# Self-attention values on 64x32 tiles in float32, outputs of a tile copied at once

## The chip, the cores and the metric

One core of a Trainium2 chip. The metric is device time in microseconds (us) of one execution of the whole kernel. Engines: PE is TensorE (PEld its weight loads), DVE is VectorE, ACT is ScalarE, POOL is GpSimd, SP is SyncE.

## What is computed

A layer over x of 32 batches x 64 tokens x 512, with a context of 32 x 512 x 384: cross-attention, causal self-attention, then a feed-forward block on half of the tokens. The change is in the second line:

```python
x = x + xattn(layernorm(x), ctx, mask, Wq, Wk, Wv, Wo)      # 16 heads of 32
x = x + attn(layernorm(x), wq, wk, wv, wo)                  # below
x = x + ffn(layernorm(x), w_router, W1, b1, W2, b2)         # top half of the tokens

def attn(x, wq, wk, wv, wo):          # 16 heads of 32, 64 queries, 64 keys
    q, k, v = heads(x @ wq), heads(x @ wk), heads(x @ wv)
    q, k = rope(q), rope(k)
    s = where(causal, q @ k.T / sqrt(32), -inf)
    return merge(softmax(s) @ v) @ wo
```

## The kernel before

Every engine has its own instruction stream, written out by hand, and they meet in semaphores. The order of the work is the order in these streams. The three blocks follow each other; their edges overlap. The self-attention works on 16 tiles of 128 tokens, two batches each. PSUM, where TensorE writes, has 8 banks (`bank[0]` to `bank[7]`).

Precision: a projection is made of three float32r products, high x high, high x low and low x high (`project`, line 955). The high part is a copy rounded to float32r (ScalarE), the low part is what is left (VectorE). The scores (`scores`, line 977) are one product in plain float32; TensorE records each such matmul twice. The values before (`values`, line 995) are float32r again: for each pair of 128-column blocks, each batch and each of the three products, the 64 rows of a batch hold 128 columns of v as the stationary operand and the probabilities of 4 heads (256 columns) move. Of the result only the part that belongs to the head is used. It lies in banks 4 to 7, where the scores are too. For this the probabilities, transposed into banks 0 and 1, are copied to `pb_h` by ScalarE and corrected to `pb_l` by VectorE (line 1225), two halves a tile; v is copied to `v_h` and corrected to `v_l` (line 1194); and the outputs are picked out head row by head row: four copies to `o_h` (32 partitions each, `outputs`, line 1083) and four corrections to `o_l` (line 1190) a tile, which the output projection (line 969) takes.

A step t of `pe3` (line 1007) holds, in this order: query projection of tile t+1 (bank 2); transposes of the rotated queries and keys of tile t (lines 1017 and 1022, banks 0 and 1); key projection of t+1 (bank 3); scores of t (banks 4 to 7); probability transposes of t-1 (line 991, banks 0 and 1); output projection of t-2 (bank 2); token transposes of t+2 (line 966, bank 3); values of t-1 (banks 4 to 7); value projection of t+1 (bank 1). In a step VectorE (`dve3`) has: value correction, two output corrections of t-2, rotation of the queries (lines 1141, 1149), rotation of the keys, mask (line 1216), two probability corrections, maximum (line 1229), residual add and statistics of t-2, token correction (line 1180), two output corrections of t-1, sum (line 1242) and reciprocal (line 1246). ScalarE (`act3`) has the copies that go with these, the layer norm (line 410) and the exponential (line 1133). GpSimd (`pool3`) has the sums of the rotation (lines 1253, 1257), subtracts the maximum (line 1262) and multiplies by the reciprocal (line 1266), which makes the probabilities.

`steps` (line 1269) runs t = 0 and 1 written out, then a hardware loop that runs a body of six steps twice, then t = 14 written out (for GpSimd also 15). In step 14 ScalarE also makes the deviations of 12 tiles (two table loads) and normalizes four tiles for the next block (`act_normalize`, line 1440). The last tile is in `pe_end`, `act_end` and `dve_end` (from line 1493): there the self-attention's last products are mixed with the beginning of the next block, which is the router's dot products (`dve_dot`), their spread over a batch (`pe_spread`, line 1459), comparison and one-hot (`dve_compare`, `dve_one_hot`), gathers of the chosen tokens (`pe_gather`, line 1468) and splits of the first feed-forward weights (`act_split`). `settle` (line 58) is an increment of a semaphore that nobody waits for, put after a wait.

## Time and profile before

| | |
|---|---|
| median of 3 runs | 1393.96 us (1391.40 to 1397.39) |
| the profiled execution | 1394.26 us |
| its span | 1392.5 us |
| busy in the span: TensorE, VectorE, ScalarE, GpSimd | 97%, 52%, 54%, 39% |
| granted TensorE clock, mean | 0.994 of full speed |
| stages in the trace (us from the span's start) | cross-attention to about 896, self-attention 896 to 1177, feed-forward from 1185 |

The profile is of one execution; its rows give busy times and, for each wait, who ended it. In the timeline a row may join several instructions; its second number then runs from the first one's start to the last one's end. TensorE's instructions overlap, so the distance between two starts is what an instruction costs, and its recorded duration is longer. In the chain of waits, pieces follow each other end to end.

### The profile page before, as it was taken

How to read it: one execution, taken by the hardware profiler on the slowest of the kernel's cores; microseconds unless marked ns; L12 is line 12 of the kernel's file. 1: busy time of each engine (PE TensorE's matmuls, PEld its weight loads, DVE VectorE, ACT ScalarE, POOL GpSimd, SP SyncE). 2: the span in 40 equal slices, each digit the busy share in tenths (PEclk: the TensorE clock that was granted, in tenths of full speed). 3: DMA queues.
4: the chain of work that ended last, by engine and by line, in shares of the span. 5: the costliest groups of instructions: out<-in, count | busy, mean ns of one | idle time of the engine just before them, and what ended most of it. 6: DMA issues, size and time to landing. Idle time of an engine off the chain costs nothing.

```text
span 1392.5 us, 32047 instructions
## 1 busy us (share of the span) xinstructions
PE 1356.0 (97%) x12344; PEld 1071.5 (77%) x12344; DVE 729.7 (52%) x1784; ACT 758.7 (54%) x1458; POOL 543.7 (39%) x284
## 2 busy tenths in 40 slices
PE   7999999999999999999999999989999997999998
PEld 5777777777777777777777777778888886878686
DVE  4244454454454444444444444468878889732323
ACT  5455665665665665665665666644444466442231
POOL 6543423323323323323324325634344334375342
PEclk9999999999999999999999999999999999999999
DMA  7011111111111111111111130100000002233131
GB/s 251 25 58 34 50 32 32 49 32 32 49 32 32 49 32 32 49 32 32 49 32 32 49 122 13 55 1 2 2 3 1 1 1 92 61 91 98 68 136 61
DMA packets 39340, 66.31 MB, mean 48 GB/s; under 512 B 4208, under 2 KB 8560, under 8 KB 39280
## 3 DMA queue, kind: packets, MB, share of 16 engines
q1 hardware_dynamic: 38848, 64.67, 14.4%
q8 instruction: 44, 0.72, 0.2%
q10 hardware_dynamic: 432, 0.79, 0.2%
q14 instruction: 16, 0.13, 0.0%
HBM read 61.25 MB, written 4.19 MB: 47 GB/s over the span
## 4 chain that ended last, share of the span: by engine, by line
PE 89%; DVE 2%; ACT 1%; issue 1%; POOL 1%; POOLq 0%; DVEq 0%; ACTq 0%
PE psum L204 38%; PE psum L958 9%; PE psum L252 8%; PE psum L1849 6%; PE psum L1820 6%; PE psum L222 5%; PE psum L240 5%; PE psum L973 3%; PE psum L261 3%; PE psum L1002 2%; PE psum L991 1%; PE psum L983 1%; PE psum L1831 1%; PE psum L1476 1%; PE psum L1022 0%
## 5 line engine op out<-in xcount | busy, mean ns | idle before, releaser
L300 ACT ACTIVATE PT<-psum 128x512 f32<-128x512 f32 x256 | 153.2, 598 | 230.0 <-PE psum L252 230.0
L287 ACT ACTIVATE prob<-prob,nmx 128x512 f32<-128x512 f32 x256 | 182.6, 714 | 94.4 <-DVE nmx L342 94.4
L356 DVE COPY V<-psum 128x512 f32<-128x512 f32 x128 | 88.6, 692 | 230.2 <-PE psum L204 230.2
L342 DVE CUSTOM_DVE_ANT_0 prob<-psum,mbias 128x512 f32<-128x512 f32 x256 | 165.5, 684 | 67.0 <-PE psum L222 67.0
L293 ACT ACTIVATE prob<-prob,rinv 128x512 f32<-128x512 f32 x256 | 182.7, 714 | 0.0
L489 POOL TENSOR_SCALAR ctx_a<-ctx_r 128x1536 fp32r<-128x1536 f32 x16 | 65.4, 4090 | 265.2 <-PE psum L204 265.0
L489 POOL TENSOR_SCALAR ctx_b<-ctx_r 128x1536 fp32r<-128x1536 f32 x16 | 65.5, 4091 | 251.6 <-PE psum L204 235.4
L252 PEld LDWEIGHTS psum<-ident,prob 128*128 128x128 f32 x1024 | 127.9, 141 | 34.6 <-issue 1.5
L252 PE MATMUL psum<-ident,prob 128*128 128x128 f32 x1024 | 153.7, 272 | 0.5 <-ACT PT L300 0.4
L204 PE MATMUL psum<-wv_h,ctx_b 128*128 128x512 f32 x384 | 144.7, 418 | 0.0
L204 PE MATMUL psum<-wv_h,ctx_a 128*128 128x512 f32 x384 | 142.2, 412 | 1.2 <-DVE K L356 1.2
L356 DVE COPY K<-psum 128x512 f32<-128x512 f32 x128 | 88.4, 691 | 96.1 <-PE psum L204 78.9
L204 PE MATMUL psum<-ctx_b,wk_h 128*128 128x512 f32 x384 | 128.3, 401 | 2.2 <-DVE x_l L1180 2.2
L204 PE MATMUL psum<-ctx_a,wk_h 128*128 128x512 f32 x384 | 127.2, 399 | 0.0
L1363 POOL TENSOR_TENSOR w_l<-w_r,w_h 128x1024 fp32r<-128x1024 f32 x32 | 77.2, 2412 | 74.0 <-ACT w_h L1358 64.7
L240 PEld LDWEIGHTS psum<-PT,V 128*32 128x32 f32 x4096 | 60.1, 110 | 51.3 <-DVE V L356 22.7
L204 PEld LDWEIGHTS psum<-ctx_b,wk_h 128*128 128x128 f32 x384 | 72.3, 188 | 19.9 <-DVE x_l L1180 2.4
L204 PEld LDWEIGHTS psum<-ctx_a,wk_h 128*128 128x128 f32 x384 | 72.0, 188 | 18.1 <-DVE V L356 0.8
L204 PEld LDWEIGHTS psum<-wv_h,ctx_a 128*128 128x128 f32 x384 | 72.2, 188 | 14.8 <-DVE K L356 1.6
L204 PEld LDWEIGHTS psum<-wv_h,ctx_b 128*128 128x128 f32 x384 | 72.5, 189 | 13.1
L204 PE MATMUL psum<-wv_l,ctx_b 128*128 128x512 f32 x192 | 75.4, 393 | 0.0
L204 PE MATMUL psum<-ctx_b,wk_l 128*128 128x512 f32 x192 | 75.4, 393 | 0.0
(225 smaller groups left out, 2968.8 us busy)
## 6 DMA issues: line engine op xcount, KB each, us to landing
ctx_r<-in_ctx SPq DMA_DIRECT2D x32, 768.0 KB, 4.6
w_r<-in_L_ffn_W SPq DMA_DIRECT2D x64, 256.0 KB, 2.8
xres<-in_x SPq DMA_DIRECT2D x16, 256.0 KB, 2.7
out<-tok SPq DMA_DIRECT2D x13, 256.0 KB, 3.7
tok<-in_x SPq DMA_DIRECT2D x3, 1024.0 KB, 12.0
...
```

Of the source, the lines that this page charges most:

```text
L204: ins = pe.matmul(KV_bank[m % 2], stat, mov, start=(c == 0 and n == 0), stop=(c == CT - 1 and n == PRODUCTS - 1))
L240: ins = pe.matmul(place[r * HD:(r + 1) * HD, c * SQ:(c + 1) * SQ], V_sb[:, b, kt, h:h + HD], PT[:, r, kt, c * SQ:(c + 1) * SQ], start=(kt ...
L252: ins = pe.transpose(T_bank[:, kt * P:(kt + 1) * P], prob[:, r, kt * P:(kt + 1) * P], ident[:])
L287: act.activation(prob[:, r, :], prob[:, r, :], ACT.Exp, bias=nmx[:, r:r + 1], scale=-1.0, accum_out=rsum[:, r:r + 1]).then_inc(s_ex, 1)
L293: act.activation(prob[:, r, :], prob[:, r, :], ACT.Copy, scale=rinv[:, r:r + 1]).then_inc(s_pn, 1)
L300: act.activation(PT[:, r, :, :].rearrange("p k n -> p (k n)"), T_bank, ACT.Copy).then_inc(s_Pt, 1)
L342: dve.tensor_tensor_reduce(prob[:, r, :], S_bank[r], mbias[:, b, :], 1.0, 3.0e38, ALU.add, ALU.min, nmx[:, r:r + 1]).then_inc(s_mx, 1)
L356: dve.tensor_copy(item_place(q, m), KV_bank[m % 2]).then_inc(s_KVe, 1)
L489: pool.tensor_scalar(y[:, 0], ctx_r[:], 1.0, None, ALU.mult).then_inc(s_cx, 1)
L958: ins = pe.matmul(b, y[:, k, :], w[:, k, :], start=(k == 0 and i == 0), stop=(k == DT - 1 and i == PRODUCTS - 1))
L1820: ins = pe.matmul(h_bank[e % 2], w[:, e, 0, k * P:(k + 1) * P], y[:, k, cols], start=(k == 0 and i == 0), stop=(k == DT - 1 and i == PRODU ...
L1849: ins = pe.matmul(y_bank[t], h[:, e % 2, t * P:(t + 1) * P], w[:, e, 1, :], start=(isinstance(f, int) and f == 0 and i == 0), stop=(isinst ...
```

## The change

The transposed probabilities and v are kept as plain float32 (`pT`, `v_s`), with one ScalarE copy each and no correction. The values of a tile become 32 float32 matmuls, one for each head and batch: the batch's 64 rows x the head's 32 columns of v are stationary, the head's 64 probability columns move, at tile position (64 b, 32 r). Consecutive matmuls alternate between the two row halves; the halves write banks 0 and 1. All four head rows of the output then hold only what is used, so one ScalarE copy and one VectorE correction of 128 partitions take the whole tile; `o_h` and `o_l` get two buffers. On TensorE the values of t-1 move from after the token transposes to right behind the scores of t, the probability transposes of t-1 move into the middle of the key projection, and the value projection into bank 1 now waits for the output correction of t-1. ScalarE copies the output before the token copy; VectorE corrects it after the maximum, and the statistics of t-2 move behind the token correction. The loop runs a body of two steps six times. In the last tile the probability transposes of tile 14 move ahead of the scores, both waiting output projections and the first spread move ahead of tile 15's probabilities, and `act_normalize(act, 1)` moves behind the exponential; the last outputs go to banks 4 and 5.

```diff
--- before.py
+++ after.py
@@ -918,31 +918,30 @@
...
-        pb_h = m("pb_h", [P, 2, 2, 4, SQ], F32R)
+        pT = m("pT", [P, 2, 4, 2, SQ], F32)
...
+        v_s = Map(nc, PT_end - 8 * 1024)("v", [P, 2, D], F32)
...
-        v_h = m("v_h", [P, 3, D], F32R)
...
-        o_h, o_l = m("o_h", [P, DT, BPG, SQ], F32R), m("o_l", [P, DT, BPG, SQ], F32R)
+        o_h, o_l = m("o_h", [P, 2, DT, BPG, SQ], F32R), m("o_l", [P, 2, DT, BPG, SQ], F32R)
...
-        pb_l, v_l = m("pb_l", [P, 2, 2, 4, SQ], F32R), m("v_l", [P, 3, D], F32R)
@@ -992,27 +991,25 @@
...
-        def values(pe, buf, h):
-
-            for n in (2 * h, 2 * h + 1):
-                cols = slice(n % 2 * 4 * SQ, (n % 2 + 1) * 4 * SQ)
-                for i, (v, p) in enumerate(((v_h, pb_h), (v_l, pb_h), (v_h, pb_l))):
+        def values(pe, buf, first_bank=0):
+
+            for n in range(DT):
+                for r in range(4):
                     for b in range(BPG):
-                        rows = slice(b * SQ, (b + 1) * SQ)
-                        ins = pe.matmul(bank[4 + 2 * b + h][:, cols], v[rows, buf, n * P:(n + 1) * P],
-                                        p[rows, h, n % 2, :, :].rearrange("p a c -> p (a c)"),
-                                        start=(i == 0), stop=(i == PRODUCTS - 1), tile_position=(b * SQ, 0))
+                        rows, h = slice(b * SQ, (b + 1) * SQ), n * P + r * HD
+                        ins = pe.matmul(bank[first_bank + b][head_rows(r), n * SQ:(n + 1) * SQ], v_s[rows, buf, h:h + HD],
+                                        pT[rows, n // 2, r, n % 2, :], start=True, stop=True,
+                                        tile_position=(b * SQ, r * HD))
             return ins
...
                 pe.wait_ge(s3_aq, t + 1)
-                if has(t - 2):
-                    pe.wait_ge(s3_pd, 2 * t - 2)
...
@@ -1022,54 +1019,50 @@
...
             if has(t + 1):
-                project(pe, bank[3], x3_h[:, nxt, :, :], x3_l[:, nxt, :, :], kw_h, kw_l).then_inc(s3_K, 1)
+                project(pe, bank[3], x3_h[:, nxt, :, :], x3_l[:, nxt, :, :], kw_h, kw_l, (0, 1))
+            if has(t - 1):
+                pe.wait_ge(s3_pn, t)
+                pe.wait_ge(s3_qa, t + 1)
+                pe.wait_ge(s3_kT, t + 1)
+                for h in range(2):
+                    probabilities(pe, nxt, h).then_inc(s3_PT, 1)
+            if has(t + 1):
+                project(pe, bank[3], x3_h[:, nxt, :, :], x3_l[:, nxt, :, :], kw_h, kw_l, (2, 3)).then_inc(s3_K, 1)
             if has(t):
                 pe.wait_ge(s3_kT, t + 1)
                 pe.wait_ge(s3_qa, t + 1)
-                at_least(pe, s3_od, 4 * t - 4)
+                at_least(pe, s3_ms, t)
                 if isinstance(t, int) and t == 0:
                     pe.wait_ge(s_x1, G + 1)
                 scores(pe).then_inc(s3_S, 1)
             if has(t - 1):
-                pe.wait_ge(s3_pn, t)
-                if has(t):
-                    pe.wait_ge(s3_qa, t + 1)
-                    pe.wait_ge(s3_kT, t + 1)
-                for h in range(2):
-                    probabilities(pe, nxt, h).then_inc(s3_PT, 1)
+                pe.wait_ge(s3_pa, 2 * t)
+                settle(pe)
+                values(pe, nxt).then_inc(s3_PV, 1)
             if has(t - 2):
                 pe.wait_ge(s3_rq, 2 * t + 4)
                 if isinstance(t, int) and t == 2:
                     pe.wait_ge(s3_wd, 1)
-                pe.wait_ge(s3_od, 4 * t - 4)
-                output_projection(pe).then_inc(s3_Wo, 1)
+                pe.wait_ge(s3_od, t - 1)
+                output_projection(pe, par).then_inc(s3_Wo, 1)
             if has(t + 2):
                 pe.wait_ge(s3_rk, 2 * t + 4)
                 pe_x(pe, t + 2, bank[3])
-            if has(t - 1):
-                pe.wait_ge(s3_v, t)
-                if has(t):
-                    pe.wait_ge(s3_ms, t + 1)
-                for h in range(2):
-                    pe.wait_ge(s3_pd, 2 * t - 1 + h)
-                    ins = values(pe, (tri - 1) % 3, h)
-                ins.then_inc(s3_PV, 1)
             if has(t + 1):
+                at_least(pe, s3_od, t)
                 project(pe, bank[1], x3_h[:, nxt, :, :], x3_l[:, nxt, :, :], vw_h, vw_l).then_inc(s3_V, 1)
...
-        def o_block(r):
-
-            src = psum[head_rows(r), 4:8, :].rearrange("p g c -> p (g c)")
-            src = src.rearrange("p (b n h q) -> p n b h q", b=BPG, n=DT, h=4)[:, :, :, r, :]
...
+        def o_block(buf, first_bank=0):
+
+            src = psum[:, first_bank:first_bank + BPG, 0:DT * SQ].rearrange("p b (n q) -> p b n q", n=DT)
+            return src, o_h[:, buf].rearrange("p n b q -> p b n q"), o_l[:, buf].rearrange("p n b q -> p b n q")
+
+        def p_place(h):
+
+            return pT[:, h].rearrange("p r c q -> p (r c q)")
@@ -1077,21 +1070,12 @@
...
             if has(t):
                 act.wait_ge(s3_V, t + 1)
-                if isinstance(t, int):
-                    at_least(act, s3_PV, t - 2)
-                else:
-                    act.wait_ge(s3_PT, 2 * t - 2)
-                copy(v_h[:, tri, :], bank[1]).then_inc(s3_vh, 1)
@@ -1108,31 +1092,28 @@
...
-            if isinstance(t, int) and t == G - 2:
-                act_deviations(act, MOST)
-                act.activation(warm[:], epsb[:], ACT.Exp)
             if has(t - 1):
                 at_least(act, s3_PV, t - 1)
                 for h in range(2):
                     act.wait_ge(s3_PT, 2 * t - 1 + h)
-                    src, high, _ = p_block(h)
-                    copy(high, src).then_inc(s3_pa, 1)
+                    copy(p_place(h), bank[h]).then_inc(s3_pa, 1)
             if isinstance(t, int) and t == G - 2:
+                act_deviations(act, MOST)
+                act.activation(warm[:], epsb[:], ACT.Exp)
                 act.wait_ge(s3_K, G)
                 act.wait_ge(s4_nm, 1)
                 act_normalize(act, 0)
+            if has(t - 1):
+                at_least(act, s3_Wo, t - 2)
+                act.wait_ge(s3_PV, t)
+                src, high, _ = o_block(1 - par)
+                copy(high, src).then_inc(s3_oa, 1)
             if has(t + 2):
                 act_x(act, t + 2, par, bank[3])
-            if has(t - 1):
-                at_least(act, s3_Wo, t - 1)
-                act.wait_ge(s3_PV, t)
-                outputs((0, 1))
             if has(t):
                 act.wait_ge(s3_su, t + 1)
                 s_ = sm[:, par].rearrange("p a b c d -> p (a b c d)")
                 act.activation(s_, s_, ACT.Exp).then_inc(s3_ex, 1)
-            if has(t - 1):
-                outputs((2, 3))
 
@@ -1181,19 +1162,20 @@
...
-            if has(t):
-                dve.wait_ge(s3_vh, t + 1)
-                dve.tensor_tensor(v_l[:, tri, :], bank[1], v_h[:, tri, :].bitcast(F32), ALU.subtract).then_inc(s3_v, 1)
-            if has(t - 2):
-                outputs(t - 2, (2, 3))
...
+        def dve_o(dve, tile, buf, first_bank=0):
+
+            src, high, low = o_block(buf, first_bank)
+            dve.wait_ge(s3_oa, tile + 1)
+            dve.tensor_tensor(low, src, high.bitcast(F32), ALU.subtract).then_inc(s3_od, 1)
@@ -1213,30 +1195,20 @@
...
-                                         .broadcast_to([P, 4, 4 * SQ]), op0=ALU.mult, op1=ALU.add).then_inc(s3_ms, 1)
-            if has(t - 1):
-                at_least(dve, s3_PV, t - 1)
-                for h in range(2):
-                    src, high, low = p_block(h)
-                    dve.wait_ge(s3_pa, 2 * (t - 1) + h + 1)
-                    dve.tensor_tensor(low, src, high.bitcast(F32), ALU.subtract).then_inc(s3_pd, 1)
-            if has(t):
...
+            if has(t - 1):
+                dve_o(dve, t - 1, 1 - par)
             if has(t - 2):
                 dve.wait_ge(s3_Wo, t - 1)
                 dve.tensor_tensor(one_tile(t - 2), bank[2], one_tile(t - 2), ALU.add).then_inc(s3_x, 1)
-                next_stats(dve, t - 2)
             if has(t + 2):
                 dve_x(dve, t + 2, par, bank[3])
-            if has(t - 1):
-                at_least(dve, s3_Wo, t - 1)
-                outputs(t - 1, (0, 1))
+            if has(t - 2):
+                next_stats(dve, t - 2)
             if has(t):
                 dve.wait_ge(s3_ex, t + 1)
@@ -1269,12 +1241,12 @@
...
-                step(eng, t, t % 2, t % 3)
-            with eng.Fori(0, (G - 4) // 6) as h:
-                for i in range(6):
-                    step(eng, 6 * h + 2 + i, i % 2, (2 + i) % 3)
+                step(eng, t, t % 2)
+            with eng.Fori(1, G // 2 - 1) as h:
+                for i in range(2):
+                    step(eng, 2 * h + i, i)
             for t in range(G - 2, end):
-                step(eng, t, t % 2, t % 3)
@@ -1501,39 +1474,35 @@
...
-            pe.wait_ge(s3_kT, G)
+            pe.wait_ge(s3_pn, LAST)
             pe.wait_ge(s3_qa, G)
-            pe.wait_ge(s3_od, 4 * (LAST - 1))
-            scores(pe).then_inc(s3_S, 1)
-            pe.wait_ge(s3_pn, LAST)
             pe.wait_ge(s3_v, G)
             for h in range(2):
                 probabilities(pe, 1 - PAR, h).then_inc(s3_PT, 1)
+            pe.wait_ge(s3_kT, G)
+            pe.wait_ge(s3_ms, LAST)
+            scores(pe).then_inc(s3_S, 1)
+            pe.wait_ge(s3_pa, 2 * LAST)
+            values(pe, 1 - PAR).then_inc(s3_PV, 1)
             pe.wait_ge(s3_x, LAST - 2)
-            output_projection(pe).then_inc(s3_Wo, 1)
-            pe.wait_ge(s3_ms, G)
-            for h in range(2):
-                pe.wait_ge(s3_pd, 2 * LAST - 1 + h)
-                ins = values(pe, (TRI - 1) % 3, h)
-            ins.then_inc(s3_PV, 1)
+            output_projection(pe, PAR).then_inc(s3_Wo, 1)
+            pe.wait_ge(s3_x, LAST - 1)
+            pe.wait_ge(s3_od, LAST)
+            output_projection(pe, 1 - PAR).then_inc(s3_Wo, 1)
+            pe_spread(pe, 0)
 
             pe.wait_ge(s3_pn, G)
             for h in range(2):
                 probabilities(pe, PAR, h).then_inc(s3_PT, 1)
-            pe.wait_ge(s3_x, LAST - 1)
-            pe.wait_ge(s3_od, 4 * LAST)
-            output_projection(pe).then_inc(s3_Wo, 1)
-            pe_spread(pe, 0)
-            for h in range(2):
-                pe.wait_ge(s3_pd, 2 * G - 1 + h)
-                ins = values(pe, TRI, h)
-            ins.then_inc(s3_PV, 1)
+            pe.wait_ge(s3_ms, G)
+            pe.wait_ge(s3_pa, 2 * G)
+            values(pe, PAR, LAST_BANK).then_inc(s3_PV, 1)
             pe_gather(pe, 0, 0)
             pe_gather(pe, 0, 1)
             pe_spread(pe, 1)
             pe.wait_ge(s3_x, LAST)
@@ -1542,40 +1511,36 @@
...
-            act_normalize(act, 1)
...
+            src, high, _ = o_block(1 - PAR)
+            copy(high, src).then_inc(s3_oa, 1)
             act.wait_ge(s3_su, G)
             last = sm[:, PAR].rearrange("p a b c d -> p (a b c d)")
             act.activation(last, last, ACT.Exp).then_inc(s3_ex, 1)
-            act.wait_ge(s3_Wo, LAST - 1)
-            act.wait_ge(s3_PV, LAST)
-            for r in range(4):
-                src, high, _ = o_block(r)
-                copy(high, src).then_inc(s3_oa, 1)
+            act_normalize(act, 1)
 
             for f in range(3):
                 act_split(act, f)
...
+                copy(p_place(h), bank[h]).then_inc(s3_pa, 1)
+            act.wait_ge(s3_Wo, LAST - 1)
+            act.wait_ge(s3_PV, G)
+            src, high, _ = o_block(PAR, LAST_BANK)
+            copy(high, src).then_inc(s3_oa, 1)
             act_normalize(act, 2)
-            act.wait_ge(s3_Wo, LAST)
-            act.wait_ge(s3_PV, G)
-            for r in range(4):
-                src, high, _ = o_block(r)
-                copy(high, src).then_inc(s3_oa, 1)
@@ -1588,40 +1553,21 @@
...
-            outputs(LAST - 2, (2, 3))
-            dve.wait_ge(s3_vh, G)
-            dve.tensor_tensor(v_l[:, TRI, :], bank[1], v_h[:, TRI, :].bitcast(F32), ALU.subtract).then_inc(s3_v, 1)
...
-            dve.wait_ge(s3_PV, LAST - 1)
-            low_probabilities(LAST - 1)
+            dve_o(dve, LAST - 1, 1 - PAR)
             add(LAST - 2)
@@ -1630,20 +1576,16 @@
...
-            dve.wait_ge(s3_Wo, LAST - 1)
-            outputs(LAST - 1, range(4))
...
             dve_diagonal(dve, 0)
-            dve.wait_ge(s3_PV, LAST)
-            low_probabilities(LAST)
...
             dve_diagonal(dve, 1)
-            outputs(LAST, range(4))
+            dve_o(dve, LAST, PAR, LAST_BANK)
...
```

## Rows read from the trace of the kernel before

**Rows 1.** The page's first part: busy time, share of the span, instructions.
```profile
PE 1356.0 (97%) x12344; PEld 1071.5 (77%) x12344; DVE 729.7 (52%) x1784; ACT 758.7 (54%) x1458; POOL 543.7 (39%) x284
```

**Rows 2.** Chain of waits, steady loop: start us, us, engine, written tile, line, count.
```profile
1033.73 5.91 PE psum L958 x24
...
1098.57 5.71 PE psum L958 x24
...
1112.67 0.44 PE psum L966 x4
...
1113.10 1.63 PE psum L1002 x24
```

**Rows 3.** Timeline, TensorE, one step: start us, us from first start to last end.
```profile
1039.91 0.60 PE L1022 MATMUL psum<-ident,k_r 128*128 128x128 f32 x4
...
1040.58 0.39 PE L958 MATMUL psum<-ak_l,x_h 128*128 128x512 f32 x1
...
1043.22 1.01 PE L983 MATMUL psum<-k_T,q_T 32*64 32x64 f32 x64
...
1044.16 1.09 PE L991 MATMUL psum<-ident,sm 128*128 128x128 f32 x8
...
1045.33 0.40 PE L973 MATMUL psum<-ao_l,o_h 128*128 128x512 f32 x1
...
1047.86 0.60 PE L966 MATMUL psum<-ident,xn 128*128 128x128 f32 x4
...
1050.36 0.39 PE L958 MATMUL psum<-av_l,x_h 128*128 128x512 f32 x1
```

**Rows 4.** Timeline, TensorE, cross-attention.
```profile
501.44 1.10 PE L240 MATMUL psum<-PT,V 128*32 128x64 f32 x64
...
502.81 0.40 PE L204 MATMUL psum<-ctx_b,wk_l 128*128 128x512 f32 x1
```

**Rows 5.** Timeline, VectorE, tiles 0 and 1.
```profile
917.85 0.69 DVE L1141 TENSOR_TENSOR r_cos<-psum,rope 128x512 f32<-128x512 f32 x1 [2.30 <-PE psum L958]
...
919.12 1.22 DVE L1216 SCALAR_TENSOR_TENSOR sm<-psum,cmask 128x1024 f32<-128x1024 f32 x1
...
920.37 1.22 DVE L1229 TENSOR_REDUCE mx<-sm 128x16 f32<-128x1024 f32 x1
...
921.50 0.68 DVE L1180 TENSOR_TENSOR x_l<-psum,x_h 128x512 fp32r<-128x512 f32 x1
...
931.84 0.69 DVE L1141 TENSOR_TENSOR r_cos<-psum,rope 128x512 f32<-128x512 f32 x1 [1.23 <-POOL q_r L1253]
```

**Rows 6.** Timeline, TensorE, start of the self-attention.
```profile
927.00 0.63 PE L1022 MATMUL psum<-ident,k_r 128*128 128x128 f32 x4 [1.14 <-DVE v_l L1194]
...
936.70 0.50 PE L958 MATMUL psum<-av_h,x_h 128*128 128x512 f32 x1
```

**Rows 7.** Timeline, ScalarE, end of the self-attention.
```profile
1142.85 2.93 ACT L1443 ACTIVATE xn<-tok,nmr,rs 128x512 f32<-128x512 f32 x4
...
1157.83 1.06 ACT L1560 ACTIVATE sm<-sm 128x1024 f32<-128x1024 f32 x1
...
1161.23 2.95 ACT L1358 ACTIVATE w_h<-w_r 128x1024 fp32r<-128x1024 f32 x3
```

**Rows 8.** Timeline, GpSimd, end of the self-attention.
```profile
1150.73 1.91 POOL L1266 TENSOR_TENSOR sm<-sm,rc 128x1024 f32<-128x1024 f32 x1 [3.20 <-DVE rc L1246]
...
1160.61 1.90 POOL L1266 TENSOR_TENSOR sm<-sm,rc 128x1024 f32<-128x1024 f32 x1 [2.81 <-DVE rc L1632]
```

**Rows 9.** Timeline, TensorE, end of the self-attention.
```profile
1152.14 1.00 PE L983 MATMUL psum<-k_T,q_T 32*64 32x64 f32 x64 [1.69 <-DVE o_l L1595]
...
1171.39 3.84 PE L1476 MATMUL psum<-oh,xn 128*128 128x128 f32 x32 [1.51 <-DVE oh L1430]
...
1177.14 0.47 PE L973 MATMUL psum<-ao_h,o_h 128*128 128x512 f32 x1 [1.48 <-DVE o_l L1595]
...
1179.98 2.25 PE L1476 MATMUL psum<-oh,xn 128*128 128x128 f32 x18
```

81 lines of the change are left out of this document (31 added, 50 removed).

## The prediction

> **What bounds the kernel now.** I read the page's first part, then the chain of waits from 890 to 1215 us (self-attention and its two seams), then each engine's timeline there. TensorE is busy for 97% of the span [rows 1]. In the chain, one tile of the steady loop is TensorE alone: 16.16 us from one value projection to the next (1098.57 to 1113.10 + 1.63), of which the values product, line 1002, holds 1.63 [rows 2]. No other engine stands in the chain from 936 to 1146 us. So in the loop only what shortens TensorE's own sequence counts. VectorE and ScalarE time that comes free is worth nothing there; it is worth something at the seams, where TensorE waits for them.
>
> **The values product.** Before: 24 matmuls of 256 columns in float32r. After: 32 matmuls of 64 columns in float32 on 64x32 tiles. A float32 matmul is recorded twice, as the scores are (64 records for 32 matmuls). Recorded durations overlap, so I work with distances from start to start.
> - Taken out: from the first token transpose (1047.86) to the second matmul of the value projection (1050.36) it is 2.50 us, with the values between [rows 3]. Straight from four transposes to a projection it is 1039.91 to 1040.58, or 0.67 [rows 3]. So 1.83 leave.
> - Put in: today it is 0.94 from the scores to the probability transposes (1043.22 to 1044.16), and 1.17 from there to the output projection's second matmul (1045.33), 2.11 in all [rows 3]. New: the eight transposes stand inside the key projection and add 0.88 (four take 0.44 in the chain [rows 2]); the split itself costs nothing more, as a projection follows transposes without a gap already. Scores to values 0.94, as to the transposes now. Values to output projection: the trace has no 64x32 tile with 64 columns. The nearest row is the cross-attention's product on 128x32 tiles, also 64 records of 64 columns: from its first to the second matmul behind it 501.44 to 502.81, or 1.37 [rows 4]. Sum 3.19, or 1.08 more.
> - Net: -0.75 us for each tile. The cheap bound is the pace of the scores, 64 columns on 32x64 tiles (0.94 to what follows and 0.32 to its second matmul: 1.26), net -0.86. The dear bound: if the two row halves didn't overlap, the 64 records, 0.88 us at the cross-attention's pace, take twice that, net +0.13. The scores alternate their row groups matmul by matmul as the new product alternates its halves, and they overlap; so I take 1.37.
> - The no-op that line 61 adds on TensorE's queue ahead of the values: at nothing, since the queue runs ahead of the array; bound 0 to +0.15 a tile.
>
> **Are the new waits covered?** Take S, the first start of the scores. VectorE has the key rotation at S+0.11, the mask at +1.38, the maximum at +2.63 and whatever follows at +3.76: so it was for tile 0, which has no probability correction between (917.85, 919.12, 920.37, 921.50 [rows 5]; its scores began at 917.74). What follows is now the one output correction, 0.69 long, which TensorE sees at about S+4.6. The value projection, which now waits for it since the outputs sit in banks 0 and 1, would start at 0.94 + 1.37 + 2.53 (1045.33 to 1047.86) + 0.35 = S+5.2. Margin 0.6 us. The probability transposes wait for ScalarE's key copy, which I put half a microsecond ahead of them. Then what goes from the other engines (two probability, one value and three output corrections on VectorE, three copies on ScalarE, per tile) is worth nothing in the loop: TensorE covered it. If that cover went, the next in line would be this same output correction.
>
> **Loop turns.** The loop of six steps jumps back once, and there the chain shows 5.91 where it has 5.71 elsewhere [rows 2]. A loop of two steps jumps back five times: 4 x 0.2 = +0.8.
>
> **Start.** TensorE waited 1.14 us for the value correction at 927.00 [rows 6]. That goes, but tile 0's probabilities are now wanted 3 us sooner than GpSimd has them, which gives about 0.95 back. What decides is the value projection of tile 2, at 936.70 [rows 6]. It now waits for mask, maximum and output correction behind a key rotation that GpSimd held until 931.84 [rows 5], or until 931.25 with VectorE free 0.6 sooner: 3.65 + 0.69 + 0.13 later is 935.7 to 936.3. I take -0.7, bound 0 to -1.0.
>
> **Steady part.** Values of tiles 1 to 12: 12 x -0.75 = -9.0.
>
> **End.** In the last loop-like step ScalarE normalizes four tiles, 2.93 us from 1142.85 [rows 7], ahead of the output copy, as before. The last value projection now waits for the correction behind that copy: about +2.0 on TensorE. It delays nothing, since GpSimd has tile 14's probabilities only at 1150.73 + 1.91 = 1152.6 [rows 8], as before. On the old clock, from there:
> - The transposes of tile 14 go first, so the last scores start at 1153.6 for 1152.14 [rows 9]. From the scores to the end of GpSimd's last multiply it was 1162.51 - 1152.14 = 10.4 [rows 8, 9]; tile 15's probabilities come at 1164.0, a loss of 1.5.
> - In exchange both output projections that stood behind them, and the first spread, are done by then. The last exponential ended at 1158.9 [rows 7]; 1.5 later comes 1160.4. Behind it ScalarE has one normalization (2.93), the weight splits (2.95 [rows 7]) and two copies (1.09), no longer four output copies: last values at 1167.5, first gather at 1168.5 for 1171.39 [rows 9].
> - Gather and spread take 4.3; comparison and one-hot, 2.8 on VectorE, then start at once, where they stood behind four output corrections for which TensorE, too, waited 1.48 at 1177.14 [rows 9]. Second gather at about 1175.8 for 1179.98 [rows 9].
> - So -4.1, bound 0 to -6, as several chains meet here. Behind it the order is unchanged.
>
> **Sum.** -0.7 - 9.0 + 0.8 - 4.1 = -13.0 us. The profiled execution took 1394.26 (span 1392.5), 0.3 above the median of 1393.96; from the median, 1381.
>
> **A rule against it.** The scores' 64 records start 12.5 ns apart, (1.01 - 0.22)/63 [rows 3]. The Trainium skill (TensorEngine Tiling (Array Packing), Performance Considerations) says that a matmul costs about 60 cycles on top however few columns it has, and advises against tiling what is small already. By an estimate from that page, 64 records take 1.6 us at 2.4 GHz, as much as the old product; the trace agrees with it only if a float32 matmul counts once.
>
> **Rivals.**
> - A floor of some 26 ns for each record: 64 x 26 = 1.66 us for 0.88. The loop then gains nothing: -0.7 + 0.4 + 0.8 - 2.5 = -2.0, 1392. Both tiled products in the trace run at half that. (The page's rule, counted per record, is this case.) Chance 0.06.
> - Partly given back: the no-op and its wait drain TensorE between scores and values (12 x 0.15 = 1.8), the start gives nothing and the end 0 to -2, since ScalarE's long normalizations stand before what TensorE needs: -9.0 + 0.8 + 1.8 and 0 to -2 are -6.4 to -8.4, 1386 to 1388. For it: that seam is decided by waits less than 1 us apart. Chance 0.24.
> - Slower: row halves that alternate don't run side by side on 64-row tiles, each record takes 55 ns and the product 3.5 us. With a product of P us the sum is 12 (P - 1.63) + 2 (P - 0.88) - 0.7 + 0.8 - 4.1 = 14 P - 25.3 (two of the products lie on the end's path): +24, 1418. It passes zero at 28 ns a record and +7 us at 36. The scores' alternation speaks against it. Chance 0.05.
>
> **How the numbers follow.** The forecast keeps 0.65. A measurement of this kernel tells about 0.5%, 7 us, from no change; the forecast and most of the partial case lie below 1387: faster 0.81. The rest of it and the floor: same 0.14. Slower 0.05. The low end takes the cheap bound (12 x 0.11) and an end of -6, 1378, with 3 us for covers I did not see; the high end is the partial case's, with 1 us for the median's own place: 1375 to 1389.
>
> **What would show it.** In the chain a period of 15.4 us with values of 0.85 to 1.05 and no VectorE line; 2 us of waiting at the last value projection; the second gather 13 us sooner. A period over 15.8, or a value projection that waits for the output correction in each tile, would make it wrong.

## The result, and the profile after

The kernel after the change takes 1378.60 us (median of 4 executions, 1377.36 to 1379.07), beside 1393.03 us of the kernel before on the same chip (1391.40 to 1397.39): a ratio of 0.989 [0.9866, 0.9914], or 14.4 us less. The forecast was 1381 in a range of 1375 to 1389. The profiled execution took 1377.36 us, its span is 1374.9, its mean granted clock 0.995.

The page's first part, kernel after (compare [rows 1]):

```profile
PE 1341.6 (98%) x12984; PEld 1059.8 (77%) x12984; DVE 666.7 (48%) x1688; ACT 730.2 (53%) x1410; POOL 544.3 (40%) x284
```

VectorE lost 63.0 us of work (729.7 to 666.7) and ScalarE 28.5, about four times and twice what the kernel won, and TensorE is as full as it was. The time was won where TensorE's own sequence became shorter. The chain of waits in the steady loop of the kernel after (start us, us, engine, written tile, line, count; compare [rows 2]):

```profile
1043.08 5.54 PE psum L957 x24
...
1049.49 1.38 PE psum L957 x6
1050.88 0.87 PE psum L990 x8
1051.75 1.40 PE psum L957 x6
1053.14 0.94 PE psum L982 x56
1054.09 0.79 PE psum L1000 x53
1054.88 2.96 PE psum L972 x12
...
1058.28 1.85 PE psum L957 x8
```

The period, from one value projection's start to the next (1043.08 to 1058.28), is 15.20 us here and 15.19 over eleven steps, for 16.16. (The view ends inside the last row's piece; whole, it is 5.54, as at 1043.08.) The chain holds TensorE alone. The values (line 1000) hold 0.79 us for 1.63. The same step in TensorE's timeline (compare [rows 3]):

```profile
1053.08 1.01 PE L982 MATMUL psum<-k_T,q_T 32*64 32x64 f32 x64
1054.02 0.86 PE L1000 MATMUL psum<-pT,v 64*32 64x64 f32 x64
1054.81 0.50 PE L972 MATMUL psum<-ao_h,o_h 128*128 128x512 f32 x1
1055.14 0.40 PE L972 MATMUL psum<-ao_l,o_h 128*128 128x512 f32 x1
...
1057.68 0.60 PE L965 MATMUL psum<-ident,xn 128*128 128x128 f32 x4
1058.03 0.48 PE L957 MATMUL psum<-av_h,x_h 128*128 128x512 f32 x1
```

Scores to values is 0.94, as predicted, so the no-op ahead of the values costs nothing. From the first value matmul to the second matmul of the output projection it is 1.12 (1054.02 to 1055.14), where the prediction took 1.37. The records start (0.86 - 0.22)/63 = 10.2 ns apart. VectorE in that step, kernel after:

```profile
1054.45 1.22 DVE L1167 SCALAR_TENSOR_TENSOR sm<-psum,cmask 128x1024 f32<-128x1024 f32 x1
1055.70 1.22 DVE L1201 TENSOR_REDUCE mx<-sm 128x16 f32<-128x1024 f32 x1
1056.84 0.68 DVE L1176 TENSOR_TENSOR o_l<-psum,o_h 128x512 fp32r<-128x512 f32 x1
```

The output correction ends at 1057.5 and the value projection, which waits for it, starts at 1058.03: the margin is about half a microsecond.

At the start of the self-attention the value projection of tile 2 waits 2.32 us for the output correction, `o_l`. VectorE's key rotation, which stands with mask and maximum ahead of that correction, waits in turn for a GpSimd sum, `q_r`, that takes 3.39 us beside VectorE's `ao_l`, where it takes 1.27 elsewhere. This slow sum is not new: in the kernel before it takes 3.39 us at the same place (the last row below). Timelines of TensorE, GpSimd and VectorE, kernel after, then GpSimd, kernel before:

```profile
934.88 0.72 PE L957 MATMUL psum<-av_h,x_h 128*128 128x512 f32 x1 [2.32 <-DVE o_l L1176]
935.40 0.63 PE L957 MATMUL psum<-av_l,x_h 128*128 128x512 f32 x1
935.83 0.63 PE L957 MATMUL psum<-av_h,x_l 128*128 128x512 f32 x1
...
927.00 3.39 POOL L1225 TENSOR_TENSOR q_r<-r_cos,r_sin 128x512 f32<-128x512 f32 x1
...
926.98 2.28 DVE L1187 TENSOR_TENSOR ao_l<-ao_r,ao_h 128x2048 fp32r<-128x2048 f32 x1
...
928.35 3.39 POOL L1253 TENSOR_TENSOR q_r<-r_cos,r_sin 128x512 f32<-128x512 f32 x1
```

The matmuls behind the wait start 0.43 us apart instead of 0.23, for eight of them: TensorE is at half clock, 1.2 GHz (the granted clock from 936 to 938 us is 0.50). TensorE's timeline at the end of the self-attention (compare [rows 9]), with one VectorE row last; the row ahead of them all is the last key projection's last matmul in the kernel before, from which the end is measured further on:

```profile
1139.85 0.40 PE L958 MATMUL psum<-ak_h,x_l 128*128 128x512 f32 x1
...
1128.66 0.40 PE L957 MATMUL psum<-ak_h,x_l 128*128 128x512 f32 x1
...
1135.62 0.50 PE L957 MATMUL psum<-av_h,x_h 128*128 128x512 f32 x1 [1.87 <-DVE o_l L1176]
...
1141.45 1.06 PE L990 MATMUL psum<-ident,sm 128*128 128x128 f32 x8 [0.35 <-ACT q_T L1512]
1142.44 1.01 PE L982 MATMUL psum<-k_T,q_T 32*64 32x64 f32 x64
...
1153.57 1.22 PE L1437 MATMUL psum<-dg,same 128*128 128x256 f32 x2 [2.20 <-DVE dg L1375]
1154.58 1.91 PE L990 MATMUL psum<-ident,sm 128*128 128x128 f32 x8
1157.28 0.85 PE L1000 MATMUL psum<-pT,v 64*32 64x64 f32 x64 [0.78 <-ACT pT L1512]
1158.05 3.84 PE L1448 MATMUL psum<-oh,xn 128*128 128x128 f32 x32
...
1165.30 3.84 PE L1448 MATMUL psum<-oh,xn 128*128 128x128 f32 x32 [0.21 <-DVE oh L1402]
...
1151.52 2.00 DVE L1375 TENSOR_TENSOR dg<-fold,s_all 128x256 f32<-128x256 f32 x1
```

**Four stretches.** For every trace I took five starts of TensorE: the query projection of tile 1 (Q1), the value projections of tiles 2, 3 and 14 (V2, V3, V14), and the first matmul of the feed-forward's second weights (FF). V3 to V14 is eleven steady steps. All later readings go by this table (us; medians of all executions in the last column, each beside a kernel before of 1392.5 to 1394.2).

| kernel | Q1-V2 | V2-V3 | V3-V14 | V14-FF | Q1-FF | median |
|---|---|---|---|---|---|---|
| before | 25.44 | 16.16 | 177.96 | 61.85 | 281.41 | 1393.03 |
| before, second trace | 25.92 | 17.19 | 177.94 | 62.04 | 283.09 | 1393.73 |
| after | 24.97 | 16.80 | 167.07 | 59.48 | 268.32 | 1378.60 |
| product alone | 23.95 | 16.93 | 169.30 | 60.15 | 270.33 | 1378.87 |
| VectorE's work back | 26.03 | 17.82 | 167.08 | 60.21 | 271.14 | 1381.12 |
| row halves in turn | 24.97 | 16.88 | 168.67 | 61.17 | 271.69 | 1382.14 |
| six-step body | 24.98 | 16.79 | 167.85 | 59.06 | 268.68 | 1378.21 |
| weights' correction later | 24.09 | 16.79 | 167.09 | 60.75 | 268.72 | 1378.36 |
| output copy ahead, step 14 | 24.98 | 17.94 | 167.05 | 61.22 | 271.19 | 1378.46 |
| both | 24.10 | 16.80 | 167.05 | 59.97 | 267.92 | 1377.56 |
| output correction later | 26.18 | 18.57 | 175.25 | 61.84 | 281.84 | 1390.18 |
| start: output ahead | 22.83 | 16.22 | 167.07 | 59.37 | 265.49 | 1376.19 |
| start: weights in step 0 | 23.76 | 15.28 | 166.65 | 59.54 | 265.23 | 1375.71 |
| values twice | 24.99 | 17.39 | 173.89 | 63.31 | 279.58 | 1387.00 |

So of the 13.1 us between the first two profiled self-attentions, 10.9 lie in the eleven steady steps, 2.4 at the end, 0.5 at the start, and 0.6 are given back from V2 to V3. The spans differ by 17.6 us; the rest lies outside the self-attention and is taken up with the last experiment.

The last stretch is the least certain one. Five kernels with the same code behind V14 (after, six-step body, weights' correction later, and the two last placings at the start) have 59.06 to 60.75 us there. Two things differ from trace to trace: how long TensorE is at half clock, and an idle time in one of the last output projections (the profile calls it "issue": no engine is named), which is 0.16 us in the kernel after, 1.48 with VectorE's work back, 1.74 with the row halves in turn and 1.56 with the output correction later. Why it differs was not tried.

### The profile page after: what moved, and what is told of

Its sections match the earlier page's. It is cut to its first block, busy times and chain, and to the rows that moved or that the text cites. A ratio compares the mean times of both kernels' runs of the same rounds, so it can differ in the third digit from the quotient of the medians.

```text
span 1374.9 us, 33152 instructions
## 1 busy us (share of the span) xinstructions
PE 1341.6 (98%) x12984; PEld 1059.8 (77%) x12984; DVE 666.7 (48%) x1688; ACT 730.2 (53%) x1410; POOL 544.3 (40%) x284
## 4 chain that ended last, share of the span: by engine, by line
PE 89%; DVE 2%; ACT 2%; issue 1%; POOL 1%; POOLq 0%; DVEq 0%; ACTq 0%
PE psum L204 39%; PE psum L957 9%; PE psum L252 8%; PE psum L1791 6%; PE psum L1762 6%; PE psum L222 5%; PE psum L240 5%; PE psum L261 3%; PE psum L972 3%; PE psum L990 1%; PE psum L1448 1%; PE psum L982 1%; PE psum L1000 1%; PE psum L1773 1%; PE psum L1019 0%
```

## Experiments

### The product alone

The kernel before with the new product and what it needs (float32 `pT` and `v_s`, one output copy and correction), in the old order: values behind the token transposes, banks 4 and 5, body of six steps.

```diff
-                for h in range(2):
-                    pe.wait_ge(s3_pd, 2 * t - 1 + h)
-                    ins = values(pe, (tri - 1) % 3, h)
-                ins.then_inc(s3_PV, 1)
+                pe.wait_ge(s3_pa, 2 * t)
+                settle(pe)
+                values(pe, nxt).then_inc(s3_PV, 1)
```

> The kernel before with the new product alone: values in float32 on 64x32 tiles, still after the token transposes (banks 4 and 5), no corrections of probabilities and v, one copy and one correction of the output; TensorE's order, the loop of six steps and the order of the last tile stay. Theory (the product's own time pays, the moves only make room for it): from the rows of the changed kernel (0.20 to the first of its 64 records, 0.79 to what follows, 0.33 to the second matmul, for 2.50 with the old product) the period is 16.16 - 0.85 = 15.3 us, and the total 9 to 13 us below the kernel before. Rival (the new order and the two-buffer outputs carry the gain, since they take waits off the loop): the period stays above 15.9 and the total gains less than 4 us.

Measured: 1378.87 us (1378.40 to 1380.84), ratio 0.9899 [0.9883, 0.9916]. Chain of waits, product alone:

```profile
1030.21 0.60 issue
...
1042.63 0.79 PE psum L1002 x53
1043.42 5.70 PE psum L959 x24
...
1053.71 1.02 PE psum L992 x8
1054.74 2.77 PE psum L974 x12
...
1058.73 3.42 PE psum L959 x14
```

The period is 15.31 (1043.42 to 1058.73; the view ends inside the last piece), so the product brings 0.85 us a tile and the new order another 0.12. The 0.60 of "issue" at 1030.21 is the jump of the six-step body; that one step is 16.17. Moving the transposes and the values trades pieces almost evenly: transposes 1.02 to 0.87 and value and query projection 5.70 to 5.54, against 2.77 to 2.96 for the output projection. By the medians the product alone is the whole gain, within what can be told; between the two profiled self-attentions (270.33 and 268.32) the other changes bring 2.0 us. The end takes 60.15 here with the old order of the last tile, for 61.85 before and 59.48 after. That lies within what kernels with the new order vary by, so no run shows that the new order of the last tile gained anything.

### VectorE's work back in

The kernel after, with two extra rotations, one token correction and three statistics a step, into spare tiles: 3.8 us more of VectorE per step, in about the places of what was removed, but nothing more ahead of the output correction than the two rotations in the query part.

```diff
+                for i in range(2):
+                    dve.tensor_tensor(spare[i][:].rearrange("p (h i) -> p h i", h=HEADS), bank[2].rearrange("p (h i) -> p h i", h=HEADS),
+                                      rope[:, 0:1, :].broadcast_to([P, HEADS, HD]), ALU.mult)
...
+                dve.wait_ge(s3_xh, t + 3)
+                dve.tensor_tensor(spare[2][:], bank[3], x3_h[:, par].rearrange("p n c -> p (n c)").bitcast(F32), ALU.subtract)
...
+            if has(t - 2):
+                for i in range(3):
+                    dve.bn_stats(spare[3 + i][:, 0:6], one_tile(t - 2))
```

> The changed kernel with as much VectorE work as the change took out of a step: six operations of 0.6 to 0.7 us on spare tiles, put where the trace shows VectorE idle (two beside the query rotation, one beside the token correction, three behind the reciprocal). Theory (VectorE's freed time is worth nothing in the loop): period 15.19 us as in the changed kernel, total within 3 us of it. Rival (the freed time is what pays): the period goes back towards 16.16, total up by up to 12 us.

Measured: 1381.12 us (1378.79 to 1381.73), ratio 0.9906 [0.9889, 0.9924]. V3 to V14 is 167.08, the same as without: in the loop this time of VectorE's is worth nothing. The 2.8 us between the traces lie at the seams: 1.1 up to V2, where TensorE waits for VectorE's rotations (1.00 and 1.16 us for 0.50 and 0.61), 1.0 to V3 (a longer stretch at half clock), and 0.7 at the end, which isn't more than that stretch varies by.

### Row halves in turn

```diff
-            for n in range(DT):
-                for r in range(4):
-                    for b in range(BPG):
+            for b in range(BPG):
+                for n in range(DT):
+                    for r in range(4):
```

> The changed kernel with the two row halves of the values one after the other (batch loop outermost), so that consecutive matmuls no longer alternate between row halves. Theory 1 (the alternation keeps 8 tiles at work; 4 tiles alone run at the cross-attention's pace): the 64 records take 0.88 us for 0.64 (13.9 ns each for 10.2), +0.25 a tile, +3 to 4 us in all. Theory 2 (a fixed cost of each matmul sets the pace, not the tiles): 0.64 as before, no change.

Measured: 1382.14 us (1381.45 to 1383.03), ratio 0.992 [0.9904, 0.9937]. Timeline of TensorE, halves in turn:

```profile
1055.51 0.99 PE L1000 MATMUL psum<-pT,v 64*32 64x64 f32 x64
1056.43 0.51 PE L972 MATMUL psum<-ao_h,o_h 128*128 128x512 f32 x1
```

The product takes 0.92 from start to start for 0.79, and a steady step 0.145 us more (168.67 - 167.07, over eleven). The records start 12.3 ns apart ((0.99 - 0.22)/63 is 12.2; over all 16 tiles the trace has 12.3) for 10.2. So neither theory holds: alternating the halves is worth half of what the first one said, and no row shows which tiles run side by side. That the total is 3.5 us up, as the first theory had it, is luck: 1.6 lie in the eleven steps, and 1.7 at the end, where TensorE has the idle 1.74 us for which no engine is named. The 55 ns a record of the third rival are far off in either order.

### The body of the loop

```diff
-            with eng.Fori(1, G // 2 - 1) as h:
-                for i in range(2):
-                    step(eng, 2 * h + i, i)
+            with eng.Fori(0, (G - 4) // 6) as h:
+                for i in range(6):
+                    step(eng, 6 * h + 2 + i, i % 2)
```

> The changed kernel with the old loop, a body of six steps run twice. As predicted (each jump back costs 0.2 us): -0.8 us, with one step of 15.4 in the trace. Rival (a jump back of the two-step body costs nothing, as the even period of 15.19 in the trace of the changed kernel says; only the long body's jump costs): +0.2, one step of 15.4, total the same.

Measured: 1378.21 us (1377.15 to 1378.91), ratio 0.9888 [0.9871, 0.9904]. Chain of waits, six-step body:

```profile
1029.58 2.77 PE psum L957 x12
1032.35 0.48 issue
1032.83 3.00 PE psum L957 x12
...
1045.48 5.54 PE psum L957 x24
```

The long body's one jump costs 0.7 us (this step is 15.90, V3 to V14 is 0.78 more); the five jumps of the short body cost nothing that shows: its steps with and without a jump all take 15.15 to 15.20, and the long body's steps without one 15.19 to 15.22. The term of +0.8 has the wrong sign. At the level of the whole kernel the two can't be told apart.

### The output correction later

VectorE makes two more such corrections (of 0.6 us each, into spare tiles) ahead of the real one.

```diff
+            for i in range(2):
+                dve.tensor_tensor(spare[i][:].rearrange("p (n b q) -> p b n q", n=DT, b=BPG), src, high.bitcast(F32), ALU.subtract)
             dve.tensor_tensor(low, src, high.bitcast(F32), ALU.subtract).then_inc(s3_od, 1)
```

> The kernel after the change, with VectorE's o_l late by two more such subtractions (into spare tiles, about 0.6 us each, 1.2 us together) ahead of the real one, in every tile. It tests the prediction's margin: it put the new wait of the value projection for o_l 0.6 us clear of being felt (the trace of the changed kernel says 0.5). If so, the value projection starts 1.2 - 0.5 = about 0.7 us late in each step: period 15.9 instead of 15.19, time +8 to +10 us, 1387 to 1389, and the chain of waits now names VectorE's o_l in the loop. If the half clock follows such waits as at the start, more: up to +20. Rival (the wait is hidden by more than I say, because the projection is not what bounds): no change. Rival (any VectorE time counts): 1.2 x 14 = +17.

Measured: 1390.18 us (1388.15 to 1394.10), ratio 0.9984 [0.9972, 0.9996]. Chain of waits, correction later:

```profile
1048.61 1.12 DVE spare L1178 x2
...
1049.84 0.65 DVE o_l L1179
...
1050.54 5.77 PE psum L958 x24
```

VectorE now stands in the loop's chain, and the period is 15.93 (175.25 / 11), 0.74 more for 1.2 us of delay: the margin was 0.46, by a test that doesn't rest on reading when a semaphore is seen. It is the nearest limit in the loop. The median lies 1 to 3 us above what I expected. In the trace 5.3 us lie outside the eleven steps: 1.2 up to V2, 1.8 to V3 (the wait there is 3.52 us, and the stretch at half clock is longer) and 2.4 at the end, part of which is the idle time with no engine named. Two instructions, 1.2 us together, in the wrong place give back 11.6 of the 14.4 us.

### Values twice

```diff
-            for n in range(DT):
+            for n, c in [(n, DT + n) for n in range(DT)] + [(n, n) for n in range(DT)]:
...
-                        ins = pe.matmul(bank[first_bank + b][head_rows(r), n * SQ:(n + 1) * SQ], v_s[rows, buf, h:h + HD],
+                        ins = pe.matmul(bank[first_bank + b][head_rows(r), c * SQ:(c + 1) * SQ], v_s[rows, buf, h:h + HD],
```

> The kernel after the change, with the 64 value matmuls of each tile made twice, the first set into PSUM columns that nobody reads. It measures the disputed term, the price of 64 more such matmuls on tiles of 64 rows by 32 columns. The prediction took 1.37 us from the first of them to the next step's second matmul, and bounds of 26 to 55 ns a matmul record; the changed kernel's trace says 0.79 from the first value matmul to the first projection matmul, 10.2 ns each by the group's own length. If the pace is what counts: +0.65 to +0.79 a tile, period 15.84 to 15.98, and 16 x 0.65 to 0.79 = +10.4 to +12.6 us, 1389 to 1391.5. Rival (the pace of 12.5 ns that the scores have): +0.8, period 15.99. Rival (an entry cost of about 0.2 us is hidden in the first set only, so that a second costs more than its length): over +0.85.

Measured: 1387.00 us (1385.90 to 1391.64), ratio 0.9957 [0.9943, 0.9971]. Chain of waits, values twice:

```profile
1044.62 1.41 PE psum L1000 x91
...
1049.43 5.54 PE psum L957 x24
...
1065.25 5.54 PE psum L957 x24
```

64 further records cost 0.62 us a step (15.81 for 15.19; 6.82 over eleven steps): 9.7 ns each, just under the low end of what I expected, and the rest of the 0.79, 0.17 us, is paid once for the group. So the disputed term is 0.62 + 0.17, not the 0.88 and more that the cross-attention's rows suggested. The median rises by 8.4 us, less than the 10.4 to 12.6 I expected, while the profiled self-attention is 11.3 longer. The profiled execution, at 1390.14, is slower than the median and has a mean granted clock of 0.995 where the median one has 0.998, so the step is read from the trace and not from the median.

### The start: three placings

First the weights' correction (`ao_l`, 2.28 us) moves in step 1 from ahead of the key rotation to behind the token correction.

```diff
             if isinstance(t, int) and t == 1:
                 shifts(dve, slice(G - 2, G), 2)
-                dve.wait_ge(s3_wa, 1)
-                dve.tensor_tensor(ow_l[:], ow_r[:], ow_h[:].bitcast(F32), ALU.subtract).then_inc(s3_wd, 1)
...
                 dve_x(dve, t + 2, par, bank[3])
+            if isinstance(t, int) and t == 1:
+                dve.wait_ge(s3_wa, 1)
+                dve.tensor_tensor(ow_l[:], ow_r[:], ow_h[:].bitcast(F32), ALU.subtract).then_inc(s3_wd, 1)
```

> The kernel after the change, with one thing moved: in step 1 VectorE subtracts the high part of the self-attention output weights (128x2048, 2.28 us) after x_l of tile 3 instead of ahead of the rotation of K. In the changed kernel that subtraction ran beside GpSimd's q_r (3.39 us), which held back r_cos, the mask, o_l and with o_l the value projection of tile 2 (a 2.32 us wait), and TensorE's next matmuls were at half clock (12 of them in 7.39 us with Q's, 5.54 in a steady step). Theory (the start gave back what the change took in the steps): the wait falls under 0.5 us, the half clock goes with it, and the time falls by 2.3 + 1.85 = about 4 us, at least 2.5: 1374.5 to 1376 where the changed kernel gives 1378.6. Rival (something else ends there next: x_l of tile 3, or the subtraction now holds back the row sum and the next step's rotation): the value projection starts sooner, but the next query projection waits instead; gain 0 to 1.5 us. Second rival: the half clock is not caused by the wait, since it stays where the wait is gone; gain about 2.3.

Measured: 1378.36 us (1375.44 to 1379.52), ratio 0.9891 [0.9874, 0.9907]. The theory missed, and neither rival had the cause. GpSimd's sum is back at 1.27 us, but the wait only fell from 2.32 to 2.11, and the half clock stayed. Timelines of VectorE and TensorE, correction later:

```profile
932.53 1.22 DVE L1167 SCALAR_TENSOR_TENSOR sm<-psum,cmask 128x1024 f32<-128x1024 f32 x1
933.78 1.22 DVE L1199 TENSOR_REDUCE mx<-sm 128x16 f32<-128x1024 f32 x1
934.91 0.68 DVE L1176 TENSOR_TENSOR o_l<-psum,o_h 128x512 fp32r<-128x512 f32 x1
...
935.65 0.50 PE L957 MATMUL psum<-av_h,x_h 128*128 128x512 f32 x1 [2.11 <-DVE o_l L1176]
```

The wait is VectorE's order. Step 1 has no output projection between the values and the value projection (2.96 us in the loop), so TensorE gets there 3 us earlier relative to VectorE, which still does mask and maximum first. What q_r gained TensorE used up by not being held at the token transposes. Up to V2 it is 0.88 us less (24.97 to 24.09).

Then, on top of that, the output correction of tile 0 goes between mask and maximum in step 1.

```diff
                 dve_mask(dve, par).then_inc(s3_ms, 1)
+                if isinstance(t, int) and t == 1:
+                    dve_o(dve, 0, 0)
...
-            if has(t - 1):
+            if has(t - 1) and not (isinstance(t, int) and t == 1):
                 dve_o(dve, t - 1, 1 - par)
```

> The kernel of the later subtraction (weights after x_l in step 1), with one thing more: in step 1 VectorE forms o_l of tile 0 between the mask and the maximum instead of after the maximum. That kernel still had a 2.11 us wait of the value projection for o_l: step 1 has no output projection between the values and the value projection (2.96 us in the loop), and VectorE reached o_l only after mask and maximum. New theory: the wait is VectorE's order, so o_l comes 1.2 us sooner, the wait falls from 2.11 to about 0.9. If the half clock behind it comes from one long wait (before the change the same place had waits of 0.87 and 1.16 with work between them and kept the full clock), it goes too, and value and query projection take 5.54 us instead of 7.38: 1.2 + 1.85 = 3.0 less than the later subtraction alone, less up to 0.7 because the maximum is late and the row sum stands behind the weights' subtraction (3.12 us): 1375.5 to 1376.5 by the median. Rival (the half clock is not the wait's doing): first 24 matmuls stay at 7.4, gain 1.2 or less, not to be told from noise by the median; then I read the chain alone.

Measured: 1376.19 us (1374.80 to 1378.64), ratio 0.9872 [0.9853, 0.9892]. The wait is 0.85, and the half clock is gone. Busy time and granted clock (the column behind GpSimd's) from 935 to 950 us, this kernel:

```profile
935.00:950.00 15.00, 14.17 (x191) 11.46 (x190) 11.64 (x14) 5.02 (x8) 6.47 (x5) 1.00 0.01 1
```

In the kernel after, the same stretch has a granted clock of 0.89. Q1 to V3 falls from 41.77 to 39.05 us, 2.7 less, and the time by 2.4 to the median. Both theories of this run hold, with a new wait of 0.83 us further on, for GpSimd's probabilities of tile 1: the weights' correction stands ahead of the row sum.

Last, the weights' correction goes to step 0, behind the token correction there.

> As the last one, but with the weights' subtraction in step 0, in VectorE's 2.6 us wait ahead of the row sum of tile 0 (it is then beside GpSimd's subtraction of the maxima, and should take 2.3 to 3.1 us, so that the row sum is up to 0.5 us late), and not ahead of the row sum of tile 1. Value projection of tile 2 to start 22.8 to 23.4 us after the query projection of tile 1 (24.81 in the changed kernel), full clock behind it, and the probabilities of tile 1 without a wait: 3 to 3.5 us less than the changed kernel, 1375 to 1375.6. Rival: GpSimd's subtraction of the maxima is the one slowed (to 3.4 us, as q_r was), the row sum is 1.5 us late, and it gives 1 us less than that.

Measured: 1375.71 us (1374.89 to 1376.83), ratio 0.987 [0.9853, 0.9886]. Q1 to V3 is 39.04, the same as in the last kernel: the probabilities of tile 1 no longer wait, those of tile 0 wait 1.66 instead of 0.76, since the correction took 3.72 us beside GpSimd's subtraction and the row sum came 0.9 us late. The correction came out dearer than the 2.3 to 3.1 us I expected, and the value projection starts 23.76 us after Q1, not the expected 22.8 to 23.4. This is still the fastest kernel of the study, 2.9 us below the changed one by the medians; the ranges, 1374.89 to 1376.83 and 1377.36 to 1379.07, don't overlap.

### The end: the output copy ahead of the normalizations

```diff
-                act.wait_ge(s3_K, G)
-                act.wait_ge(s4_nm, 1)
-                act_normalize(act, 0)
             if has(t - 1):
                 at_least(act, s3_Wo, t - 2)
                 act.wait_ge(s3_PV, t)
                 src, high, _ = o_block(1 - par)
                 copy(high, src).then_inc(s3_oa, 1)
+            if isinstance(t, int) and t == G - 2:
+                act.wait_ge(s3_K, G)
+                act.wait_ge(s4_nm, 1)
+                act_normalize(act, 0)
```

> The kernel after the change, with one thing moved: in step 14 ScalarE copies the output of tile 13 before its four normalizations (2.92 us) instead of after them. The prediction said that the wait of the last value projection (measured 1.87 us, and the 12 matmuls behind it in 4.62 us instead of 2.77 for the half clock) delays nothing, since what ends last there is a chain of ScalarE, VectorE and GpSimd. If that step holds: the wait goes, the value projection ends 3 to 3.7 us sooner, and the time stays within 0.7 us of 1378.6. Rival (the end is bound by TensorE as the loop is, and the scores of tile 15 were held by it): the time falls by 2.5 to 3.7 us, to 1375 to 1376. Between them: part of it, 1 to 2 us, if the normalizations, now about 0.6 us later, hold exp of tile 14.

Measured: 1378.46 us (1375.95 to 1380.08), ratio 0.9892 [0.9875, 0.9908]. The last value projection starts without a wait and 1.8 us sooner, and the probabilities of tile 14 then wait instead. Timeline of TensorE, copy ahead:

```profile
1141.49 1.13 PE L990 MATMUL psum<-ident,sm 128*128 128x128 f32 x8 [2.57 <-POOL sm L1239]
```

So the 1.87 us wait of the changed kernel delays nothing, as the prediction said: behind it stands GpSimd's multiply for tile 14. Both moves together:

> Both moves together (the subtraction of the output weights after x_l in step 1; the output copy of tile 13 ahead of the normalizations in step 14). The two places are 200 us apart and share nothing, so the two gains should add up: by the theory of the start alone 1374.5 to 1376; where the end gives too, 1371.5 to 1373.5. If the sum is not reached, one of the two gains is taken back by the cold clock or at the join with the feed-forward part.

Measured: 1377.56 us (1373.47 to 1379.07), ratio 0.9883 [0.9865, 0.9902]. V14 to FF is 59.97 with both and 61.22 with the copy alone, for 59.48 in the changed kernel. The start's 0.9 is there, the end gives nothing. The median is above both ranges I had given.

### The kernel before, once more

> The kernel before the change, unaltered, for a second trace. In the first trace its feed-forward stage took 199.8 us from the first matmul of the second weights to the end, with a half-clock stretch at 1291 us from the start; in all eleven traces of kernels with the new product that stage took 196.6 to 196.7. The self-attention alone explains 13.1 us between the two traces, the medians differ by 14.4. If the stretch belongs to one execution (my theory: the instructions of that stage are the same): about 196.7 here as well, self-attention 281.4 from the query projection of tile 1 to that matmul. If it belongs to the kernel (the stage starts with other waits, or DMA times that differ): 199.8 again, and then the change is worth up to 3 us outside the self-attention.

Measured: 1393.73 us (1391.83 to 1395.71), ratio to the other runs of it 1.0003 [0.9988, 1.0017]. FF to the end takes 196.7 us; in the traces of the new product it is 196.6 to 196.7. The 199.8 of the first trace (its stretch at half clock after 1290 us) belonged to that execution. Q1 itself starts anywhere from 909.7 to 912.0 us in the fourteen traces, with the same code ahead of it, so the 1.35 us between the first two traces there say nothing about the change. This second trace has a half-clock stretch of its own where the first had none. Busy time and granted clock from 935 to 950 us, kernel before, second trace:

```profile
935.00:950.00 15.00, 14.80 (x142) 12.38 (x143) 10.83 (x18) 6.47 (x11) 5.74 (x4) 0.89 0.00 1
```

It has the same waits there as the first (0.87 and 1.16 us, ahead of and behind the token transposes), and lost 1.0 from V2 to V3. So these two waits bring the half clock in one execution and not in another. With a wait over 2 us it came in all ten traces that have one. In neither of the two traces with 0.85 or 0.86 there did it come, though one of them has a wait of 1.66 us some 6 us earlier.

## Why the prediction was right, point by point

- **TensorE's sequence bounds the loop; freed time on VectorE and ScalarE is worth nothing there.** Right. For VectorE it is shown: putting 3.8 us of work a step back left the eleven steps at 167.08 us. It holds for those places only; ahead of the output correction 1.2 us cost 0.74. ScalarE's work was not put back, so for it the chain, which holds TensorE alone, is the evidence.
- **Values product, -0.75 a tile.** Right in kind, too small: -0.97. What leaves (1.83) and what is added ahead (transposes inside the key projection, 0.87 in the chain for 0.88, and the split itself free; 0.94 from the scores) were as worked out. The step that was mis-sized is "values to output projection, 1.37", taken from the cross-attention's product on 128x32 tiles [rows 4]: it is 1.12, and the records' pace is 9.7 to 10.2 ns where that row has 14.0. Even the cheap bound, the scores' pace at 1.26, was too dear. Over twelve tiles, from V2 to V14, that is -11.6 for -9.0.
- **No-op ahead of the values, at nothing.** Right: 0.94 as ahead of the transposes before.
- **The output correction is next in line, margin 0.6.** Right: 0.5 by the trace, 0.46 by the delayed correction, and it then stood in the chain as said.
- **Loop jumps, +0.8.** Wrong: 0, and the 0.2 of the old body's jump is gone, -0.2 together. The price of a jump was read off one place of a body of six steps and carried to a body of two. The short body's jumps don't show, and the long body's would have cost 0.7 with the new order (0.86 with the product alone).
- **Start, -0.7.** V2 came 0.5 us sooner, inside the bound of 0 to -1.0, and by the chain that was named: GpSimd's sum, rotation, mask, maximum, output correction. What the prediction left out is the clock. Before, TensorE waited 0.87 us ahead of the token transposes and 1.16 behind them, with the values product still to come; now it is 0.61 and 2.32, and the matmuls behind the longer wait ran at half clock, which cost 1.6 us from V2 to V3 against a steady step. How much of that is the change's isn't settled, as the kernel before loses 1.0 there in one of its two traces. That the placing decides is shown: with the wait at 0.85 the start is 2.7 us shorter.
- **End, -4.1 from the last key projection to the second gather.** It is -3.5 (from 1128.66 to 1165.30 is 36.64; before, 40.13). The last scores were predicted 1.5 us later, counted from the last key projection, and are 1.5 later. The wait of the last value projection, predicted +2.0 and delaying nothing, is 1.87 and delays nothing. What failed is "the first spread is done by then": VectorE's `dg` took 2.00 us instead of 0.42 beside GpSimd's multiply, the spread waited for it (2.20), and tile 15's probabilities stood behind the spread at half clock: 1154.58 where 1152.8 was predicted (1164.0 less the 11.19 by which the last key projection comes sooner). Of these 1.8 us, 0.4 are GpSimd's multiply itself (it ended at 1153.2). Two thirds came back further on. Which part of the end the new order won isn't shown: with the old order and the new product the whole stretch is 60.15 for 59.48, and it varies by more than that.
- **The rivals.** The floor of 26 ns a record is out: 9.7 to 10.2 measured. The Trainium skill (TensorEngine Tiling (Array Packing), Performance Considerations) has about 60 cycles for every matmul, by an estimate from that page 25 ns at 2.4 GHz; here a float32 matmul, two records, costs 19.4, so the trace is below the page's figure even if it is counted once. The 55 ns a record for row halves that don't run side by side are out too, though they run at 12.3 ns even one half after the other. "Partly given back" was half true: from Q1 to V3 nothing was won (41.77 us for 41.60), as it said, and the end gave 2.4 for its 0 to 2; but the no-op cost nothing and the product more than covered the rest.
- **Sum.** -13.0 was predicted and 13.1 lie between the first two traces' self-attentions, by errors that cancel: -2.6 in twelve tiles and -1.0 at the jumps; +1.6 behind V2, +0.2 at the start and +1.7 at the end. Of this last, 0.9 lies ahead of the last key projection, 0.6 between it and the second gather and 0.2 behind. As for the 0.9: tile 14's step takes the probabilities' transposes in before that point and the values out behind it, which the prediction's clock for the end did not count. Against the second trace of before it is 14.8. The medians give 14.4, so the true size lies nearer to that, 1.4 beyond the forecast.
